# A four-layer attention and FFN program: spline weights made by GpSimd in the attention before, and the spline stage in another order

## The chip, the cores and the metric

The program runs on one core of one Trainium2 chip. A core has TensorE (PE), VectorE (DVE), ScalarE (ACT), GpSimd (POOL) and SyncE (SP, which here only issues DMA transfers). The metric is device time in microseconds; lower is better. All tiles that matter here are fp32.

## The reference

Eight sequences of 100 tokens of 512 pass through four layers, each a cross-attention over 361 context rows and an FFN. What the change touches is in layers 0 to 2:

```python
# layer 0 FFN: 16 experts of width 352, top 4 of 16, capacity 256
mid = silu(einsum('ech,ehi->eci', xg, w_gate)) * einsum('ech,ehi->eci', xg, w_up)
eout = einsum('eci,eih->ech', mid, w_down) * wbuf[..., None]
# layer 1 attention: 16 heads, q and output projections with 8-bit rows
# layer 1 FFN: three 2048 x 512 weights, each a cubic spline through 8134 control points
w = 0.5 * (2*p1 + (p2-p0)*f + (2*p0-5*p1+4*p2-p3)*f**2 + (3*p1-p0-3*p2+p3)*f**3)
inter = silu(x @ gate_w.T) * (x @ up_w.T)
return inter @ down_w.T
# layer 2 FFN: weights rounded to fp8 in blocks of 32
q = (blocks / scales).astype(float8_e4m3fn); return q * scales
```

## The kernel before

Each stage is a block in which every engine has its own program, written out by hand; semaphores order the engines. At a block's end all engines meet. No planner is involved: the order in the code is the order on the engine, and SP's DMA issues wait in one queue like any other instruction.

**Experts (`stage_L0_experts`).** 16 experts of 256 rows make 32 units of 128 rows. TensorE runs for unit u: `gate(u + 1)`, `turn_mid(u)`, `up(u + 1)`, `turn_x(u + 2)`, `down_part(u)`. VectorE makes `product(u)`, which `turn_mid(u)` waits for, and `result(u)`. Besides, the class `Triples` rounds the weights of layer 2's FFN to fp8: 16 triples (768 KB each, two halves each). `scales(n)` (VectorE) needs the loaded triple; GpSimd scales the half, `rounding(n)` is VectorE's, GpSimd's `finish` multiplies back, SP stores the triple to memory. Eight triples are done here, one half in each of units 0 to 15, the others in the column FFN. In units 16 to 23 VectorE quantizes attention weights (`rows8.vector`). SP loads expert 1's weights, the attention's constants (`rows8.sync`: four weights of 1 MB, two contexts, two masks, biases), three triples, and then follows the experts.

**Second attention (`stage_L1_attention`).** A loop over 8 batches. TensorE works on batch b and makes the keys and values of batch n = b + 1 in between: `scores(b, 1)`, `turn_heads(b, 0)`, `keys(n, 0)`, ... `keys(n, 0)` waits for the context tile `cx[n % 2]` (722 KB). SP loads `cx[b]` once the values of b - 2 are made and GpSimd has multiplied that context by the row weights (`multiplied`), then the mask. GpSimd in batch b: negate the next mask, `prod`, bias, four gathers of a later batch's expert rows, and `root(b + 2)`, which waits for VectorE's `measure(b + 2)` near the batch's end. `rows8.w` is free by then.

**Spline stage (`stage_L1_ffn`).** The down weight is made in natural order in four parts of four strips: GpSimd multiplies points by powers, TensorE multiplies by tables (`made`), ScalarE copies one side (`laid`), VectorE lays the other over it (`w_made`, `beyond_border`), SP stores it, and when all is stored GpSimd gathers sixteen strips in another row order. VectorE also measures the eight sequences and normalizes them to `xn`; TensorE transposes these (columns of x, `xT`) and multiplies them by a basis (`moments`). Gate and up weights come from eight tiles of taps: VectorE makes gate's (`gate_weights`), GpSimd up's (`up_weights`), with two tap buffers loaded by SP.

**Column FFN (`stage_columns_ffn`).** Two halves of 400 tokens, 16 chunks of hidden columns each. TensorE runs `gate_up(n)` for a pair of chunks and `down_part` two pairs behind; ScalarE makes `silu`, VectorE `product`. Between them VectorE and GpSimd round the other eight triples, a half per pair. At the half, `turn_y(0)` transposes the result and VectorE's `add` adds it; the summaries of the next layer's recurrence are made there too.

## Time and profile before

| | |
|---|---|
| Median of 3 runs | 2425.5 us (2421.78 to 2426.56) |
| Profiled execution, its own time | 2420.43 us |
| Its span in the trace | 2418.3 us |
| TensorE busy | 2228.2 us (92%), granted clock 0.951 in the mean |
| VectorE busy | 1337.7 us (55%) |
| ScalarE busy | 773.5 us (32%) |
| GpSimd busy | 762.1 us (32%) |
| DMA | 212.69 MB, 88 GB/s in the mean |

The span runs from the first to the last instruction; 2.1 us of the execution's time lie around it. In it the experts stage runs from about 677 to 966 us, the second attention to 1284, the spline stage to 1377 and the column FFN to 1525. A busy share is a mean over stages; what a change in one stage is worth is read from that stage.

### The profile page before, as it was taken

The page shows a single profiled execution, that of the slowest core. Times are in us where ns is not written, and L with a number is a line of the kernel's source. Part 1 is how long each engine was busy: PE and PEld are TensorE (multiplying, and loading weights), DVE is VectorE, ACT ScalarE, POOL GpSimd, SP SyncE. Part 2 cuts the span into 40 slices and gives each one's busy share as a digit, 9 for nine tenths or more (in the row PEclk, how much of TensorE's full clock was granted, in tenths as well). Part 3 has the DMA queues.
Part 4 walks back from the last instruction along what each step waited for, and adds up shares of the span by engine and source line. Part 5 has one row for each costly group of instructions (what it writes and reads, how often), then busy time and mean ns, then how long its engine had stood idle before and what let it go on. Part 6 is the DMA issues. An engine that isn't in the chain of part 4 may idle for free. (4 is left out here: it accounts for less than half of the span.)

```text
span 2418.3 us, 29406 instructions
## 1 busy us (share of the span) xinstructions
PE 2228.2 (92%) x10009; PEld 1178.9 (49%) x10009; DVE 1337.7 (55%) x3440; ACT 773.5 (32%) x2045; POOL 762.1 (32%) x760
## 2 busy tenths in 40 slices
PE   8999999998969999999996498799998899999899
PEld 4455555555436565555553254544443444444454
DVE  5544344206318741476766268867663455555897
ACT  1134344314001111455552111511110456645433
POOL 3655455203203300432112533400000355656100
PEclk9999999998989999899996699999999899999899
DMA  6025300005267853211004622620002211211000
GB/s 199 1 82 187 125 17 13 1 1 161 77 221 262 301 211 120 83 55 32 31 1 152 236 104 92 217 90 5 9 5 67 73 44 52 61 39 48 16 14 15
DMA packets 97353, 212.69 MB, mean 88 GB/s; under 512 B 19060, under 2 KB 37908, under 8 KB 95416
## 3 DMA queue, kind: packets, MB, share of 16 engines
q1 hardware_dynamic: 89784, 193.51, 23.4%
q0 software_dynamic: 7424, 17.32, 2.5%
q8 instruction: 82, 1.34, 0.2%
q14 instruction: 63, 0.52, 0.1%
HBM read 155.70 MB, written 50.14 MB: 85 GB/s over the span
## 5 line engine op out<-in xcount | busy, mean ns | idle before, releaser
L3839 POOL TENSOR_SCALAR a_p<-a_p,a_li 100x257 f32<-100x257 f32 x252 | 188.3, 769 | 110.5 <-DVE a_li L3702 110.5
L633 POOL TENSOR_SCALAR a_shared<-a_shared,a_li 128x361 f32<-128x361 f32 x104 | 131.7, 1266 | 182.4 <-DVE a_li L541 182.4
L3457 PE MATMUL bank<-l_early,a_ctx 128*128 128x512 f32 (+1 forms) x384 | 180.2, 615 | 0.0
L3457 PEld LDWEIGHTS bank<-l_early,a_ctx 128*128 128x128 f32 (+1 forms) x384 | 68.8, 188 | 85.0 <-issue 85.0
L313 PE MATMUL bank<-a_wk,a_ctx 128*128 128x512 f32 (+1 forms) x192 | 94.7, 614 | 9.0 <-DMA a_wk<-in_L_xattn_Wk 5.6
L691 ACT ACTIVATE a_shared<-a_shared,a_nm 128x361 f32<-128x361 f32 x104 | 62.1, 597 | 98.9 <-DVE a_nm L535 98.9
L2721 PE MATMUL bank<-f_h,s_w 128*128 128x400 f32 x256 | 93.2, 519 | 0.0
L2376 ACT ACTIVATE f_sg<-bank 128x512 f32<-128x512 f32 x25 | 14.9, 597 | 238.1 <-PE bank L2159 221.7
L313 PE MATMUL bank<-a_wv,a_ctx 128*128 128x512 f32 (+1 forms) x192 | 90.7, 592 | 0.0
L396 PE MATMUL bank<-a_q_o,a_wq_wo 128*128 128x400 f32 x256 | 88.4, 500 | 0.6 <-issue 0.6
L2326 POOL TENSOR_TENSOR f_rstd<-f_var,half 128x1 f32<-128x1 f32 (+1 forms) x12 | 7.1, 591 | 259.6 <-DVE f_var L2231 259.6
L1295 PE MATMUL bank<-e_wd,e_midT 128*128 128x512 f32 (+1 forms) x192 | 87.9, 593 | 0.6 <-ACT e_midT L1332 0.6
L1559 PE MATMUL bank<-w_ctx,w_wk 128*128 128x361 f32 x256 | 88.2, 489 | 0.0
L2185 PE MATMUL bank<-s_wd,f_hT 128*128 128x512 f32 x192 | 87.4, 599 | 0.0
L1567 PE MATMUL bank<-w_wv,w_ctx 128*128 128x512 f32 (+1 forms) x192 | 87.0, 598 | 0.0
L328 PE MATMUL bank<-a_wq_wo,a_shared 128*128 128x512 f32 x192 | 86.5, 593 | 0.0
L2159 PE MATMUL bank<-s_wgu,f_xT 128*128 128x512 f32 x192 | 84.6, 593 | 0.7 <-ACTq L2366 0.7
L533 DVE MEMSET a_hold<- 1x1 f32 x104 | 6.1, 59 | 141.6 <-PE bank L366 125.4
L2159 PE MATMUL bank<-s_wgu,s_lead 128*128 128x512 f32 x192 | 84.4, 592 | 0.0
L1275 PE MATMUL bank<-e_wu,e_xT 128*128 128x352 f32 x256 | 82.8, 467 | 0.0
L1266 PE MATMUL bank<-e_wg,e_xT 128*128 128x352 f32 x256 | 81.1, 459 | 0.2 <-ACT e_xT L1320 0.2
L1931 ACT ACTIVATE a_p<-a_p,a_nm 100x361 f32<-100x361 f32 x128 | 74.7, 588 | 13.0 <-DVE a_nm L1773 13.0
(498 smaller groups left out, 4863.9 us busy)
## 6 DMA issues: line engine op xcount, KB each, us to landing
slots_x<-zero SPq DMA_DIRECT2D x4, 4096.0 KB, 27.0
s_whole<-in_L_ffn_w SPq DMA_DIRECT2D x24, 512.0 KB, 3.7
e_wg<-in_L_ffn_w_gate SPq DMA_DIRECT2D x16, 704.0 KB, 5.7
e_wu<-in_L_ffn_w_up SPq DMA_DIRECT2D x16, 704.0 KB, 7.9
e_wd<-in_L_ffn_w_down SPq DMA_DIRECT2D x16, 512.0 KB, 4.3
e_xg<-slots_x SPq DMA_DIRECT2D x16, 512.0 KB, 5.4
slots_y<-e_y SPq DMA_DIRECT2D x32, 256.0 KB, 4.6
a_ctx<-in_ctxT SPq DMA_DIRECT2D x30, 256.0 KB, 3.1
```

What stands on the lines that cost most here:

```text
L313: mm = nc.tensor.matmul(R.bank(name, b, c)[0:m, :], cx[:, kc, lo:lo + m], w[:, kc, :], start=(kc == 0), stop=(kc == KC - 1))
L328: mm = nc.tensor.matmul(bank[:], xnT[:, kc, t * P:(t + 1) * P], wq[:, kc, n * D:(n + 1) * D], start=(kc == 0), stop=(kc == KC - 1))
L396: mm = nc.tensor.matmul(R.bank("y", half, m)[:, 0:BY_HALF * S], wo[:, h, m * P:(m + 1) * P], qo[:, half * BY_HALF:(half + 1) * BY_HALF, h, ...
L633: pool.tensor_scalar(p[s % NP], p[s % NP], li[:, b % 2, h:h + 1], None, ALU.mult).then_inc(normed, 1)
L1295: mm = nc.tensor.matmul(b_y[:], midT[u % 2][0:n, c, :], wd[e % 2][0:n, c, :], start=(c == 0), stop=(c == len(IC) - 1))
L1559: mm = nc.tensor.matmul(R.bank("k", b, n)[:, 0:T], wks[:, kc, n * P:(n + 1) * P], cx[b % 2][:, kc, :], start=(kc == 0), stop=(kc == KC - 1))
L1567: mm = nc.tensor.matmul(R.bank("v", b, c)[0:m, :], cx[b % 2][:, kc, lo:lo + m], wvs[:, kc, :], start=(kc == 0), stop=(kc == KC - 1))
L2159: mm = nc.tensor.matmul(banks[u % 2][:], xT[i % 2][:, n, kc, :], w[:, kc, j * D:(j + 1) * D], start=(kc == 0 and n == 0), stop=(kc == KC - ...
L2185: mm = nc.tensor.matmul(b_y[i % 2][:], hT[u % 2][:, n, kc, :], down[:, j * KC + kc, :], start=(j == 0 and kc == 0 and n == 0), stop=(j == ...
L2721: mm = nc.tensor.matmul(b_y[d][:, 0:GT], down[:, f, d * P:(d + 1) * P], h[m % 4][:], start=(f == 0), stop=(f == FC - 1))
L3457: mm = nc.tensor.matmul(bank[0:m, :], columns[:, kc], w[:, kc, :], start=(kc == 0), stop=(kc == KC - 1))
L3839: pool.tensor_scalar(p[g % 2][j][:, lo:hi], p[g % 2][j][:, lo:hi], li[:, h, i:i + 1], None, ALU.mult) \
```

## The change

Four things are edited. (1) GpSimd makes the gate and up weights of the spline FFN in the second attention, one tile of taps in each batch, in `rows8.w`; SP loads the taps, stores the results to memory, and in the spline stage one DMA of 1 MB loads them. (2) The spline stage's order is: measure, normalize, transposes, basis products, and then the down weight. Eight of the sixteen gathers are issued in it and the block doesn't wait for their landing; the other eight are issued by GpSimd at the start of the column FFN, whose `down_part` waits for them by groups of four. (3) Ten triples, not eight, are rounded in the experts stage, in units 4 to 15 and 24 to 31; their loads begin after expert 0, and `scales(0)` stands behind unit 3. (4) At the half of the column FFN `gate_up(PAIRS + 1)` stands ahead of `turn_y(0)`, and two `silu` ahead of `copy_y(0)`. The lines that move the table products behind the basis products on TensorE and ScalarE (the same loops, with a wait for `moved` in part 0), the semaphores and the tile declarations are left out here.

```diff
@@ -1217,8 +1218,6 @@
                 load_gate_up(1)
                 load_down(1)
                 rows8.sync(sp, *weights8)
-                for t in range(3):
-                    triples.load(sp, t)
                 for e in range(NE):
                     more = e + 2 < NE
                     if more:
@@ -1231,11 +1230,16 @@
-                    if 1 <= e <= EARLY_TRIPLES:
-                        triples.store(sp, e - 1)
-                        if e + 2 < EARLY_TRIPLES:
-                            triples.stored(sp, e - 1)
-                            triples.load(sp, e + 2)
+                    if e == 0:
+                        for t in range(3):
+                            triples.load(sp, t)
+                    if e in STORES_AFTER:
+                        t = STORES_AFTER[e]
+                        triples.store(sp, t)
+                        if t + 3 < EARLY_TRIPLES:
+                            triples.stored(sp, t)
+                            triples.load(sp, t + 3)
+                triples.store(sp, EARLY_TRIPLES - 1)
                 for i in range(2):
                     sp.wait_ge(stored[i], 16 * NE)
                 for t in range(EARLY_TRIPLES - 3, EARLY_TRIPLES):
@@ -1358,16 +1362,18 @@
                     dve.tensor_copy(y[u % 2][:], b_y[:]).then_inc(y_made, 1)
 
                 step = Link(dve, stepped)
-                triples.scales(dve, step, 0)
                 product(0)
                 for u in range(U):
                     if u + 1 < U:
                         product(u + 1)
                     result(u)
-                    if u < triples.n:
-                        if u + 1 < triples.n:
-                            triples.scales(dve, step, u + 1)
-                        triples.rounding(dve, step, u)
+                    if u + 1 == ROUNDING_UNITS[0]:
+                        triples.scales(dve, step, 0)
+                    if u in ROUNDING_UNITS:
+                        n = ROUNDING_UNITS.index(u)
+                        if n + 1 < triples.n:
+                            triples.scales(dve, step, n + 1)
+                        triples.rounding(dve, step, n)
@@ -1524,6 +1530,11 @@
+        free = rows8.w[:].rearrange("p i c n -> p (i c) n")
+        by = [free[:, i, :] for i in range(2)]
+        taps = [[free[:, 2 + 2 * i + w, :].rearrange("p (m o) -> p m o", m=4) for w in range(2)] for i in range(2)]
+        taps_in, taps_out = [sem(f"taps_in{i}") for i in range(2)], [sem(f"taps_out{i}") for i in range(2)]
+        spline_made, pool_stepped = sem("spline_made"), sem("pool_steps")
@@ -1540,13 +1551,33 @@
             def _(sp):
+
+                def load_taps(t):
+                    if t >= 2:
+                        sp.wait_ge(taps_out[t % 2], t // 2 * 32)
+                    sp.dma_start(by[t % 2], spline_by[t].rearrange("p m o -> p (m o)")).then_inc(taps_in[t % 2], 16)
+                    for w in range(2):
+                        sp.dma_start(taps[t % 2][w], spline_taps[w, t]).then_inc(taps_in[t % 2], 16)
+
+                def store_weights(t):
+                    sp.wait_ge(spline_made, 2 * t + 2)
+                    for w in range(2):
+                        sp.dma_start(spline_weights[:, w, t, :], taps[t % 2][w][:, 0, :]).then_inc(taps_out[t % 2], 16)
+
+                load_taps(0)
+                load_taps(1)
                 for b in range(2, B):
-
+                    store_weights(b - 2)
+                    load_taps(b)
                     sp.wait_ge(*R.full("v", b - 2, 2))
                     sp.wait_ge(multiplied, b - 1)
                     sp.dma_start(cx[b % 2][:], ctxT[b]).then_inc(c_in[b % 2], 16)
                     sp.wait_ge(maxed, (b - 1) * NH)
                     sp.dma_start(m_in[b % 2][:], mask[b]).then_inc(mk_in[b % 2], 16)
+                for t in range(TILES_W - 2, TILES_W):
+                    store_weights(t)
+                for i in range(2):
+                    sp.wait_ge(taps_out[i], TILES_W // 2 * 32)
@@ -1879,6 +1910,16 @@
+                step = Link(pool, pool_stepped)
+
+                def interpolate(t):
+                    pool.wait_ge(taps_in[t % 2], (t // 2 + 1) * 48)
+                    for w in range(2):
+                        a = taps[t % 2][w]
+                        step(pool.tensor_tensor(a, a, by[t % 2].rearrange("p (m o) -> p m o", m=4), ALU.mult))
+                        step(pool.tensor_tensor(a[:, 0:2], a[:, 0:2], a[:, 2:4], ALU.add))
+                        pool.tensor_tensor(a[:, 0, :], a[:, 0, :], a[:, 1, :], ALU.add).then_inc(spline_made, 1)
@@ -1903,6 +1944,7 @@
                         gather(b + 4)
                     if b + 2 < B:
                         root(b + 2)
+                    interpolate(b)
 
@@ -2573,7 +2616,9 @@
-EARLY_TRIPLES = 8
+EARLY_TRIPLES = 10
+ROUNDING_UNITS = [*range(4, 16), *range(24, 32)]
+STORES_AFTER = {t + 3 if t < 6 else t + 7: t for t in range(EARLY_TRIPLES - 1)}
@@ -2717,8 +2762,10 @@
+                    if m < FC and f % QUADS == 0:
+                        pe.wait_ge(down.arrived[f // QUADS], QUADS * 16)
@@ -2755,9 +2803,9 @@
-                turn_y(0)
                 pe.wait_ge(all_copied, 1)
                 gate_up(PAIRS + 1)
+                turn_y(0)
                 for n in range(PAIRS + 2, 2 * PAIRS + 1):
@@ -2786,8 +2834,10 @@
+                silu(FC)
+                silu(FC + 1)
                 copy_y(0)
-                for m in range(FC, 2 * FC):
+                for m in range(FC + 2, 2 * FC):
                     silu(m)
@@ -2826,42 +2877,58 @@
+                for f in range(FC // 2, FC):
+                    down.gather(pool, f)
                 triples.pool(pool)
@@ -2877,88 +2944,46 @@
-                    def load_taps(t):
-                        if t >= 2:
-                            for n in range(2):
-                                sp.wait_ge(taps_used[n], t - 1)
...
+                        down.store(sp, N * t, N * (t + 1))
+
+                    sp.dma_start(basis[:], w_in["spline_basis"]).then_inc(basis_in, 16)
                     sp.dma_start(tm[:], w_in["spline_terms"]).then_inc(c_in, 16)
                     for t in range(3):
                         load_part(t)
-                    for t in range(2):
-                        load_taps(t)
-                    sp.dma_start(basis[:], w_in["spline_basis"]).then_inc(basis_in, 16)
-                    sp.dma_start(order[:], w_in["spline_order"]).then_inc(basis_in, 16)
+                    sp.dma_start(down.order[:], w_in["spline_order"]).then_inc(order_in, 16)
                     load_part(3)
-                    store_part(0)
-                    load_taps(2)
-                    store_part(1)
-                    load_taps(3)
-                    store_part(2)
-                    load_taps(4)
-                    store_part(3)
-                    for t in range(5, TILES_W):
-                        load_taps(t)
+                    sp.dma_start(weights[:], spline_weights).then_inc(weights_in, 16)
+                    for t in range(PARTS_W):
+                        store_part(t)
...
-                    def up_weights(t):
...
+                    for b in range(B):
+                        root(b)
                     for t in range(PARTS_W):
                         pool.wait_ge(p_in[t % 3], (t // 3 + 1) * 32)
                         pool.tensor_tensor(pts[t % 3][:], pts[t % 3][:], pw[t % 3][:], ALU.mult).then_inc(multiplied, 1)
-                        root(2 * t)
-                        root(2 * t + 1)
-                    for t in range(TILES_W):
-                        up_weights(t)
-                    pool.wait_ge(basis_in, 32)
-                    pool.wait_ge(natural_out, PARTS_W * 16)
-                    for f in range(FC):
-                        pool.indirect_dma_start(wd[:, f, :], None, natural[:, :],
-                                                bass.IndirectOffsetOnAxis(ap=order[:, f:f + 1], axis=0)).then_inc(down_in, 16)
-                    pool.wait_ge(down_in, FC * 16)
+                    pool.wait_ge(order_in, 16)
+                    pool.wait_ge(down.stored, PARTS_W * 16)
+                    for f in range(FC // 2):
+                        down.gather(pool, f)
...
-                    pe.wait_ge(c_in, 16)
...
-                        pe.wait_ge(laid if b < N else w_made, (PARTS_W - 1) * N + b % N + 1)
@@ -3012,24 +3049,14 @@
-                    def gate_weights(t):
...
-                    for t in range(PARTS_W):
-                        measure(2 * t)
-                        measure(2 * t + 1)
-                        beyond_border(t)
+                    for b in range(B):
+                        measure(b)
                     for b in range(B):
                         normalize(b)
-                    for t in range(TILES_W):
-                        gate_weights(t)
-
-        stage_columns_ffn(k, "f1", weights, wd, xT, moments, raw, rounded, early, recurrence)
+                    for t in range(PARTS_W):
+                        beyond_border(t)
+
+        stage_columns_ffn(k, "f1", weights, weights_in, down, xT, moments, raw, rounded, early, recurrence)
```

## Rows read from the trace of the kernel before

**Rows 1.** Busy time by stretch, the second attention; us from the span's start, then length.
```profile
1000.00:1284.00 284.00, 265.81 (x1972) 151.32 (x1972) 190.35 (x599) 154.62 (x448) 68.20 (x50) 0.97 0.11 34
```

**Rows 2.** TensorE's longest waits: line, releaser, us in total, times, longest.
```profile
PE bank L2698 <- PEq L2865: 33.3, 1, 33.3
PE bank L1284 <- DVE e_mid L1352: 22.7, 1, 22.7
```

**Rows 3.** Timeline of TensorE, experts: start, length, instructions.
```profile
682.88 2.53 PE L1266 MATMUL bank<-e_wg,e_xT 128*128 128x352 f32 x8
...
715.87 2.53 PE L1266 MATMUL bank<-e_wg,e_xT 128*128 128x352 f32 x8
...
723.96 2.53 PE L1266 MATMUL bank<-e_wg,e_xT 128*128 128x352 f32 x8
```

**Rows 4.** Timelines of VectorE and TensorE, start and end of the experts.
```profile
706.14 0.95 DVE L2618 TENSOR_REDUCE e_top<-e_triple 128x24 f32<-128x768 f32 x1 [29.73 <-DMA e_triple<-in_L_ffn_triples]
...
716.68 0.94 DVE L2618 TENSOR_REDUCE e_top<-e_triple 128x24 f32<-128x768 f32 x1
...
721.36 0.96 DVE L2629 TENSOR_TENSOR e_v<-e_v,e_c 128x768 f32<-128x768 f32 x1
...
961.80 0.69 DVE L1358 COPY e_y<-bank 128x512 f32<-128x512 f32 x1 [3.05 <-PE bank L1295]
...
965.65 2.00 PE L1470 MATMUL bank<-ident,w_wide 128*100 128x128 f32 x8 [3.88 <-PEq L1195]
```

**Rows 5.** DMA issues: size each and median us from issue to landing.
```profile
rounded<-e_triple SPq DMA_DIRECT2D x8, 768.0 KB, 6.6
...
rounded<-f_triple SPq DMA_DIRECT2D x8, 768.0 KB, 3.2
...
w_ctx<-in_ctxT SPq DMA_DIRECT2D x8, 722.0 KB, 4.1
...
out<-l_early SPq DMA_DIRECT2D x6, 256.0 KB, 2.0
```

**Rows 6.** Timelines of GpSimd and TensorE, `root(7)` and `keys(7, 0)` of the second attention.
```profile
1212.76 0.57 POOL L1880 TENSOR_TENSOR a_rstd<-a_var,half 100x1 f32<-100x1 f32 x1 [24.81 <-DVE a_var L1739]
...
1223.54 2.67 PE L1559 MATMUL bank<-w_ctx,w_wk 128*128 128x361 f32 x8
```

**Rows 7.** The taps' instructions on GpSimd: ns min/median/max, first and last start.
```profile
L2923 POOL TENSOR_TENSOR s_taps<-s_taps,s_by x8: 1260/1772/1781, 1310.2 to 1349.7; 128x512 f32<-128x512 f32 x8
L2924 POOL TENSOR_TENSOR s_taps<-s_taps x8: 722/724/787, 1311.5 to 1351.5; 128x256 f32<-128x256 f32 x8
L2925 POOL TENSOR_TENSOR s_u<-s_taps x8: 452/455/805, 1312.3 to 1352.3; 128x128 f32<-128x128 f32 x8
```

**Rows 8.** Stretches behind TensorE's restart: the third number from the end is the granted clock.
```profile
965.00:967.00 2.00, 1.35 (x6) 1.38 (x7) 0.17 (x1) 1.37 (x2) 0.62 (x1) 0.50 0.00 0
...
971.00:973.00 2.00, 2.00 (x7) 1.22 (x6) 0.00 (x0) 0.99 (x3) 1.70 (x2) 0.84 0.57 146
```

**Rows 9.** Timelines of the spline stage, and the gathers' first and last start.
```profile
1285.54 0.69 DVE L2990 BATCH_NORM_STATS2 s_stats<-res 100x6 f32<-100x512 f32 x1 [1.64 <-PEq L80]
...
1286.55 0.68 DVE L2990 BATCH_NORM_STATS2 s_stats<-res 100x6 f32<-100x512 f32 x1
...
1309.59 2.56 DVE L3012 COPY_PREDICATED s_w<-s_beyond,bank 128x512 f32<-128x512 uint8 x4
...
1321.46 22.55 PE L2966 MATMUL bank<-s_xT,s_basis 128*128 128x400 f32 x64
...
L2938 POOL DMA_INDIRECT s_w<-spline_down,s_order x16: 944/946/1069, 1353.1 to 1372.0; - x16
```

**Rows 10.** Timeline of VectorE in the column FFN, its first rounding and the half.
```profile
1386.90 0.50 DVE L2626 TENSOR_SCALAR f_c<-f_v 128x768 int32<-128x768 int32 x1
...
1453.01 2.46 DVE L2807 TENSOR_TENSOR res<-res,bank 100x512 f32<-100x512 f32 x4
```

**Rows 11.** The gathers of the second attention: ns min/median/max.
```profile
L1874 POOL DMA_INDIRECT a_got<-slots_y,slots_of x32: 1007/1012/1507, 966.4 to 1119.6; - x32
```

## Prediction on record

> **What bounds the kernel now.** I read the busy time by stretch first, then TensorE's waits, then the timelines where they are long. TensorE is the bound: it is 92% busy on the page, and in the second attention it works 265.8 of 284.0 us at a granted clock of 0.97 while VectorE, ScalarE and GpSimd have room [rows 1]. So only what stops TensorE, or starts it later, costs time. Its two longest waits are both in stages that the change touches: 33.3 us ahead of the first column product of the spline FFN, and 22.7 us at the first expert's `turn_mid(0)` [rows 2]. The reader should ask of each part: does it take one of these away, and what is late next.
>
> **Triples in the experts stage: start.** VectorE's first instruction there is `triples.scales(0)`, ahead of `product(0)`, and it sits idle 29.73 us until the first triple lands at 706.14 [rows 4]; TensorE stands behind it. The change puts `scales(0)` after unit 3 and the triple loads after expert 0. Nothing then holds `product(0)`. `gate(1)` began at 682.88 and a unit lasts 723.96 - 715.87 = 8.09 us, so `gate(2)` begins at 690.97 in place of 715.87 [rows 3]: -24.9 us (22.7 of wait and 2.2 of slow restart). What is late next are transfers. From the sizes in the code, 9.5 MB went ahead of VectorE's 706.14 (expert 1's weights 2.16 MB, the attention's constants 6.6, one triple 0.79), which is 324 GB/s over 29.4 us. Expert 2's rows and gate/up weights now make 10.7 MB: 33 us, so 709.7 against a need at 682.9 + 3 x 8.09 = 707.2 (or later loads, behind the three triples, 16.3 MB: 727 against 723.3). The rate there was no better than this mean, but the small constants may have pulled it down. Between 0 and 5 us; I take +1, since most of these are wide rows.
>
> **Triples in the experts stage: end.** `ROUNDING_UNITS` now ends with unit 31, so VectorE rounds after the last tiles. Before, `result(31)` ran at 961.80 and all engines restarted at 965.65 [rows 4]. One `scales` and `rounding` take 721.36 + 0.96 - 716.68 = 5.6 us [rows 4]. The idle of 3.05 us in that row says that VectorE's `result(30)` ended at 958.7; `scales(19)` and `rounding(18)` push `result(31)` to 964.4 to 965.0; `rounding(19)` (4.1 us of the 5.6) ends at 969.2; GpSimd's `finish`, a 128x768 product, is 1.3 to 1.9 us by the 128x512 one that runs alone in 1.26 [rows 7], 1.5 taken: 970.7; the store of 768 KB lands in 3.2 us at the median [rows 5], which with issue and the block's end makes 975.2. That is +9.5 us. Bounds: +8.5, and +13 at 6.6 us, the median of the same store amid this stage's loads [rows 5]. TensorE idles through it, so its restart is slow in both kernels alike.
>
> **The second attention.** GpSimd gets `interpolate(b)` after `root(b + 2)`: six instructions, each half 1.26 to 1.78, 0.72 and 0.45 us [rows 7], so 5.4 to 6.2 with their steps; 5.6 taken. GpSimd has room, and the DVE instructions that it can slow have slack. But SP's loop is one queue, and ahead of the load of `cx[b + 2]` it now waits for the weights of tile b, stores them, waits until both stores landed, and issues three taps loads. Behind that wait stand `cx[b + 2]` and the mask. Count from `root`: 1212.76 + 0.57 = 1213.33 [rows 6]. Interpolation: 1218.9. Two stores issued in 0.4 us steps, the second landed 2.0 us later (the nearest row, an output store of 256 KB [rows 5]): 1221.4. Three loads issued, then the context load, issued at 1222.8; alone it lands in 4.1 us [rows 5]: 1226.9, and with 768 KB of taps just ahead 1227.4. `keys(b + 2, 0)` wants it at 1223.54 [rows 6]. TensorE waits 3.9 us; bounds 3.0 and 5.4. The delay doesn't shrink by itself: the next `measure` and `root` come after a product that TensorE runs behind these keys, so they move with the wait. Six loads are of this kind (batches 2 to 7). Before, that load had to wait only for `prod`, at the batch's start.
>
> After an idle of 3.9 us TensorE restarted at a granted clock of 0.50, the lower of its levels (1.2 of 2.4 GHz), and was back between 971 and 973 (mean 0.84), some 5.7 us later [rows 4, 8]. Half speed for 4 to 5.7 us of work costs 2.0 to 2.9; I take 2.2 (the row's wait is as long as mine; nothing if the wait is shorter than whatever drops it). So 6 x (3.9 + 2.2) = +36.6 us; 6 x 3.0 = 18 below, 6 x (5.4 + 2.9) = 50 above.
>
> **The spline stage.** Before: tables, then columns of x, then the products with the basis, which end at 1321.46 + 22.55 = 1344.0; then TensorE waits for GpSimd's and VectorE's taps and sixteen gathers, 1.26 us apart (1353.1 to 1372.0) [rows 9, 2]. Now: eight `measure` at 1.01 us from 1285.54 end at 1293.6; columns and transposes take what they took (1312.1 to 1321.5, 9.4 us) and perhaps 1 more beside GpSimd's products: 1304; basis products to 1326.6; the first tables 2 us; four copies of a part 2.56 us, sixteen 10.2 and hand-overs [rows 9]: 1340. The stores of 4.2 MB and the 1.3 MB of weights and borders share the queue from 1332; at 324 GB/s they need 17 us: 1349. Eight gathers: 1359. The block then ends without waiting for them, TensorE starts at 1359.3 against 1377.3: -18 us. If the stores drain a third faster it is -22; if the chain is longer by two gathers, -15. The removed taps (8 of each engine and 24 loads) are inside this number, and the single load of the finished weights is long landed.
>
> **The column FFN.** GpSimd issues eight gathers (10 us) ahead of `triples.pool`, so `rounding(0)`, before at 1386.90, 9.6 us after the start [rows 10], can begin only at 11.5, and the products behind it on VectorE with it; TensorE had little slack: +1.6 (0 to 4). At the half, `gate_up(PAIRS + 1)` now stands ahead of `turn_y(0)`: VectorE's `add` began at 1453.01 [rows 10] right after the summaries and now waits for those 1.6 us and the copy: +2.4, as the wait for `silu` that follows is behind these adds and a rounding. Two triples fewer save nothing: in the last pairs TensorE is back to back. +4 together.
>
> On these gathers a rule speaks against the change. The slowest of the 32 gathers of the second attention took 1.51 us beside a median of 1.01 [rows 11]. The Trainium skill (SBUF — State Buffer, section SBUF: two separate sides) says that a GpSimd-issued DMA is starved of descriptors while VectorE holds the shared port, and gives 0.62 us growing to about 3.1. This row shows a growth of half, not fivefold, so the trace bears it out only weakly.
>
> **Sum.** -24.9 + 1 + 9.5 + 36.6 - 18 + 4 = +8.2 us on the profiled execution's 2420.4, 2428.6. That execution is 5.1 us under the median 2425.5 of the runs, so in runs: 2434.
>
> **Rivals.** (1) The other side: the waits in the attention are at their lower bound, 3.0 us, and too short for the clock to fall. Then 18 in place of 36.6: -10.4, 2415. It decides at 6 x (wait + clock) = 28.4, that is 4.7 us a batch. For it: all but 0.9 us of the wait hangs on durations taken near their middle. Against it: the row with 3.9 us of idle fell. (2) The context loads are not late at all, because stores and taps overlap more than I think: -28.4, 2397. Against it: the window between `root` and need is 10.2 us, and interpolation and one landing already take 9.7. (3) Everything slow: 5.0 us waits with 2.9 of clock (47), experts' loads 5 late: +23, 2448. For it: the queue's taps are ahead of the context. (4) Gathers in the column FFN starved by VectorE as by the rule, all eight at the slowest one's 1.51 us and a gap of 0.3 [rows 11]: 4.5 us more before `rounding(0)`, +12.7, 2438. Against it: VectorE has little to do in those first 10 us. By the page's factor of five they would take 40 us, and the time would be some 2464.
>
> **Chances.** Forecast 0.50, its own range 2427 to 2441; (1) 0.27; (2) 0.06; (3) 0.13; (4) 0.04. From 2410 to 2452 holds all but (2) and the far ends of (1) and (3). A measurement tells 0.2%, 4.9 us, from no change. Faster: (2), most of (1), a little of the forecast: 0.27. Same: the lower part of the forecast and the rest of (1): 0.22. Slower: 0.51.
>
> **What would show it.** In the new profile: no wait of TensorE at `turn_mid(0)`; 8 to 13 us idle of all engines at the end of the experts; at each `keys(n, 0)`, n = 2 to 7, a wait of 3 to 5 us ended by the context load, and a granted clock of 0.5 behind it; the column FFN's start 15 to 22 us nearer to the attention's end. The prediction is wrong if those keys don't wait, or if the load runs ahead of the taps.

## The result, and the profile after

| | before | after |
|---|---|---|
| Median of 4 runs each | 2425.5 us (2421.78 to 2426.56) | 2449.3 us (2446.47 to 2453.24) |
| Profiled execution / its span | 2420.43 / 2418.3 us | 2446.47 / 2444.0 us |
| TensorE busy, granted clock | 2228.2 us, 0.951 | 2237.5 us, 0.952 |

The changed kernel takes 1.0097 times as long (95% interval 1.0079 to 1.0115): 23.8 us slower, where the prediction said 8.2. The page doesn't show it: TensorE's busy time grew by 9 us, and the mean clock is the same. The stages do. Each row of this table is one profiled execution, cut at the same events: TensorE's first product of the experts, its first of the second attention, VectorE's first `measure` of the spline stage, TensorE's first of the column FFN, the first transpose of its `turn_y(1)`, and the end.

| us | experts begin | experts | attention | spline | column FFN | rest |
|---|---|---|---|---|---|---|
| before | 678.0 | 287.6 | 319.9 | 91.8 | 144.3 | 896.7 |
| after | 682.5 | 275.1 | 365.0 | 78.8 | 145.9 | 896.8 |
| difference | +4.5 | -12.5 | +45.1 | -13.0 | +1.6 | +0.1 |
| predicted | 0 | -14.4 | +36.6 | -18 | +4 | 0 |

TensorE's longest waits in the changed kernel (line, releaser: us in total, times, longest) answer to [rows 2]:

```profile
PE bank L1590 <- DMA w_ctx<-in_ctxT: 27.7, 6, 5.3
PE bank L2743 <- PEq L2932: 25.1, 1, 25.1
PE bank L2983 <- DVE s_xn L3041: 16.5, 4, 15.9
PE bank L1476 <- PEq L1196: 12.4, 1, 12.4
```

The 22.7 us at `turn_mid(0)` are gone and the 33.3 us are 25.1. In their place stand six waits for a context, and 12.4 us at the attention's first product where 3.88 stood. Those two grew by 27.7 + 8.6 us against the 22.7 + 8.2 that went, which would be 5.4 us slower; a wait's price is more than its length, as the clock will show. The third line is the start of the spline stage in its new order.

**Experts.** TensorE's timeline of the changed kernel (start, length, instructions, idle before), which answers to [rows 3] and the last of [rows 4]:

```profile
687.34 2.53 PE L1270 MATMUL bank<-e_wg,e_xT 128*128 128x352 f32 x8
...
695.42 2.53 PE L1270 MATMUL bank<-e_wg,e_xT 128*128 128x352 f32 x8
...
703.50 2.53 PE L1270 MATMUL bank<-e_wg,e_xT 128*128 128x352 f32 x8
...
711.49 0.66 PE L1258 MATMUL bank<-ident,e_xg 128*128 128x128 f32 x4 [2.76 <-DMA e_xg<-slots_x]
...
715.33 1.13 PE L1270 MATMUL bank<-e_wg,e_xT 128*128 128x352 f32 x3 [0.60 <-issue]
...
957.59 2.00 PE L1476 MATMUL bank<-ident,w_wide 128*100 128x128 f32 x8 [12.45 <-PEq L1196]
```

`gate(2)` follows `gate(1)` after 8.08 us: the whole 24.9 us are won. Then one wait comes, for expert 2's rows; the next `gate` is at 715.33, not 711.58 (703.50 + 8.08), so it costs 3.75. At the end all engines stand still for 12.45 us, where they stood for 3.88.

**Attention.** GpSimd, SP and TensorE around the second of the late contexts:

```profile
1065.52 0.57 POOL L1911 TENSOR_TENSOR a_rstd<-a_var,half 100x1 f32<-100x1 f32 x1 [15.68 <-DVE a_var L1770]
...
1070.79 0.46 POOL L1921 TENSOR_TENSOR w_w<-w_w 128x128 f32<-128x128 f32 x1
...
1071.27 0.81 SPq L1565 DMA_DIRECT2D spline_weights<-w_w  x2
1073.40 0.33 SPq L1558 DMA_DIRECT2D w_w<-in_spline_by  x1
1073.77 0.92 SPq L1560 DMA_DIRECT2D w_w<-in_spline_taps  x2
1074.79 0.37 SPq L1574 DMA_DIRECT2D w_ctx<-in_ctxT  x1
...
1081.78 4.67 PE L1590 MATMUL bank<-w_ctx,w_wk 128*128 128x361 f32 x8 [5.35 <-DMA w_ctx<-in_ctxT]
```

Read it as a chain: root, interpolation (5.2 us), stores (0.8) and their landing (1.3), three loads of taps, the context's issue, and 7.0 us later the keys that waited for it. The same keys took 2.67 us before [rows 6] and take 4.67 here. The stretches behind the wait say why (the third number from the end is the granted clock):

```profile
1082.00:1084.00 2.00, 2.00 (x4) 1.20 (x5) 0.00 (x0) 0.00 (x0) 2.00 (x2) 0.50 0.00 0
1084.00:1086.00 2.00, 2.00 (x5) 1.09 (x5) 0.00 (x0) 0.00 (x0) 2.00 (x2) 0.55 0.00 0
1086.00:1088.00 2.00, 2.00 (x32) 1.38 (x31) 0.98 (x2) 0.56 (x1) 1.49 (x3) 1.00 0.00 0
```

TensorE is busy all the time, but at the lower of its levels (0.50, 1.2 of 2.4 GHz). The same stands behind the shortest of the six waits, 3.50 us ahead of the keys at 1124.72, where the clock is 0.50 from 1124 to 1130:

```profile
1126.00:1128.00 2.00, 2.00 (x5) 1.12 (x4) 0.00 (x0) 0.00 (x0) 2.00 (x1) 0.50 0.00 0
```

**Spline stage.** Timelines of VectorE, GpSimd, TensorE and SP in the changed kernel; the first `measure` is at 1322.54:

```profile
1331.16 4.06 DVE L3041 TENSOR_SCALAR s_xn<-res,s_stat,s_rstd 100x4 f32<-100x4 f32 x1
1335.14 0.54 DVE L3039 TENSOR_SCALAR s_xn<-res,s_stat,s_rstd 100x512 f32<-100x512 f32 x1
1335.71 0.29 DVE L3041 TENSOR_SCALAR s_xn<-res,s_stat,s_rstd 100x4 f32<-100x4 f32 x1
...
1331.50 3.70 POOL L2972 TENSOR_TENSOR s_points<-s_points,s_powers 128x512 f32<-128x512 f32 x3
...
1335.28 1.71 PE L2983 MATMUL bank<-ident,s_xn 100*128 100x100 f32 x8 [15.95 <-DVE s_xn L3041]
...
1370.95 6.85 SPq L2896 DMA_DIRECT2D spline_down<-s_w  x4
...
1397.06 0.95 POOL L2899 DMA_INDIRECT s_w<-spline_down,s_order  x1 [0.30 <-issue]
...
1401.33 1.70 PE L2743 MATMUL bank<-s_xT,s_gate_up 32*128 32x400 f32 x4 [25.09 <-PEq L2932]
```

An instruction on 100x4 elements takes 4.06 us, its twin 0.29: it begins 0.34 us before the record of GpSimd's three products and ends with the last of them, at 1335.2. The last gather of the stage ends at 1398.0, TensorE's column products start 3.3 us later.

**Column FFN.** GpSimd's last gather, VectorE's first rounding and TensorE behind the half:

```profile
1410.99 0.95 POOL L2899 DMA_INDIRECT s_w<-spline_down,s_order  x1 [0.30 <-issue]
...
1413.48 1.82 DVE L2671 TENSOR_SCALAR f_c<-f_v 128x768 int32<-128x768 int32 x1 [2.09 <-issue]
...
1472.16 3.60 PE L2791 MATMUL bank<-l_early,l_u 128*8 128x512 f32 x8
...
1488.43 1.71 PE L2743 MATMUL bank<-s_xT,s_gate_up 32*128 32x400 f32 x8 [8.38 <-ACT f_sg L2824]
```

Rounding starts 12.2 us after the stage, not 9.6 [rows 10]. From the summaries to the wait's end are 16.3 us; before they were 13.9 (1448.76 to 1462.63).

### The profile page after: what moved, and what is told of

The parts are those of the page before. It is cut to its first block and busy times, and to the rows that moved or that the text cites. A ratio compares the mean times of both kernels' runs of the same rounds, so it can differ in the third digit from the quotient of the medians.

```text
span 2444.0 us, 29422 instructions
## 1 busy us (share of the span) xinstructions
PE 2237.5 (92%) x10009; PEld 1186.7 (49%) x10009; DVE 1316.4 (54%) x3424; ACT 773.8 (32%) x2045; POOL 776.2 (32%) x784
## 5 line engine op out<-in xcount | busy, mean ns | idle before, releaser
L1590 PE MATMUL bank<-w_ctx,w_wk 128*128 128x361 f32 x256 | 100.0, 541 | 27.7 <-DMA w_ctx<-in_ctxT 27.7
L2688 POOL TENSOR_TENSOR e_v<-e_triple,e_inv 128x768 f32<-128x768 f32 x20 | 33.1, 1654 | 206.8 <-DVE e_inv L2665 206.8
L1590 PEld LDWEIGHTS bank<-w_ctx,w_wk 128*128 128x128 f32 x256 | 53.5, 220 | 59.5 <-DMA w_ctx<-in_ctxT 28.7
L534 DVE MEMSET a_hold<- 1x1 f32 x104 | 6.1, 59 | 141.5 <-PE bank L367 125.4
```

Source lines behind the costliest of these rows:

```text
L1590: mm = nc.tensor.matmul(R.bank("k", b, n)[:, 0:T], wks[:, kc, n * P:(n + 1) * P], cx[b % 2][:, kc, :], start=(kc == 0), stop=(kc == KC - 1))
```

## The experiments

Twelve runs were made, in four groups on four chips, each beside runs of the kernel before on the same chip; ratios are against those, and are what can be compared between groups. "The length of a stage" is that of the table above.

### Is it the context's place in SP's queue?

```diff
                 for b in range(2, B):
-                    store_weights(b - 2)
-                    load_taps(b)
...
                     sp.dma_start(m_in[b % 2][:], mask[b]).then_inc(mk_in[b % 2], 16)
+                    store_weights(b - 2)
+                    load_taps(b)
```

> The changed kernel with one edit: in the second attention SP loads the context and the mask of batch b ahead of the stores of the finished weights and the loads of taps. Theory 1 (the context stands behind the taps in SP's queue): the waits of TensorE at keys(2..7, 0), 27.7 us in 6, go altogether; the clock stays up behind them, so TensorE's busy time in the stage falls by some 10 of the 14.4 us that it grew; the stage shrinks from 363.9 to 322 to 328 us, and the time from 2449.3 to 2409 (2403 to 2415). Theory 2 (GpSimd's interpolation itself slows the other engines at the shared port): the waits at the keys go but others of 2 to 3 us a batch on VectorE's results come in their place: 2420 to 2430. Theory 3 (the slow clock is not due to these waits): only the 27.7 us go, 2421.

Measured: 2403.13 us, ratio 0.9896 (0.9878 to 0.9914): the changed kernel with this one edit is faster than the kernel before. The attention is 322.7 us, and no wait for a context is left. Busy times of the whole stage, first of the changed kernel, then of this one (PE is the first number after the length):

```profile
957.59:1322.54 364.95, 310.71 (x2096) 176.87 (x2096) 194.57 (x631) 165.89 (x468) 121.39 (x112) 0.91 0.18 54
```

```profile
957.86:1280.52 322.66, 297.13 (x2096) 170.18 (x2096) 208.54 (x631) 165.96 (x468) 122.70 (x112) 0.95 0.21 61
```

The queue order costs 42.3 us: 28.7 of idle time and 13.6 in which the same 2096 matmuls ran slower, 2.3 us for each of the six waits. Theories 2 and 3 fall: no other wait of that size came in place of these, and the slow clock went with them. What GpSimd's work costs by itself is the rest to the kernel before, 322.7 - 319.9 = 2.8 us.

The second kernel puts the context between the stores and the taps, so that it waits for the interpolation and not for the landing:

```diff
                     store_weights(b - 2)
-                    load_taps(b)
...
                     sp.dma_start(m_in[b % 2][:], mask[b]).then_inc(mk_in[b % 2], 16)
+                    load_taps(b)
```

> The changed kernel with one edit: SP stores the finished weights of batch b - 2 first, then loads context and mask of batch b, then waits for the stores and loads the taps. The context's issue comes earlier by the stores' landing and three issues, some 3.1 us, and has no taps in flight ahead. Theory 1: the wait at the keys falls from 4.6 us to 1 to 2 us each, 6 to 12 us in all, and so short a wait leaves TensorE's clock up: busy time as in the run with the context first, and the time 6 to 12 us above that run, some 2418. Rival (the clock falls behind any wait): the same waits but 2 to 3 us of slow clock each, some 2430. Rival (the transfer itself is slow here, not its place in the queue): waits stay at 4 us or more, 2440 or above.

Measured: 2411.31 us, ratio 0.9926 (0.9908 to 0.9943), 8.2 above the run with the context first. The waits of TensorE in the attention, and the whole stage:

```profile
PE bank L1590 <- DMA w_ctx<-in_ctxT: 4.7, 6, 1.5
```

```profile
953.96:1283.30 329.34, 297.74 (x2096) 170.23 (x2096) 198.01 (x631) 165.95 (x468) 123.98 (x112) 0.95 0.20 59
```

Six waits of 0.8 us in the mean, the longest 1.5, and a busy time that is 0.6 us off that of the run without waits: behind none of them does the granted clock leave 1.00, while the wait of 5.35 us had some four us of work at half clock behind it and the one of 3.50 more than five. The prediction's rival (1) had waits of 3.0 us without a slow clock. That short waits can go without one is shown for 0.4 to 1.5 us; at 3.0 us no context wait was measured, and the nearest, 3.50, had the slow clock. Nor is the length of the wait all that decides, as the attention's end will show.

### The experts' stage by itself

The kernel before with the hunks of the experts stage (and the guard `if n < triples.n` in the column FFN) and nothing else.

> The kernel before with the edits of the experts stage alone (loads of triples after expert 0, scales(0) behind unit 3, ten triples in units 4 to 15 and 24 to 31, six left for the column FFN). Theory 1 (the terms add): no wait at turn_mid(0), some 12 us idle at the stage's end, the stage 276.4 us in place of 288.9, nothing gained in the column FFN: 2425.5 - 12.5 = 2413. Rival 1: the stage ahead (routing), which came 4.5 us later in the changed kernel, belongs to this edit or to the program's length: 2417 to 2418. Rival 2: six triples in place of eight free VectorE and GpSimd in the column FFN and give 3 us or more: 2410.

Measured: 2412.5 us, ratio 0.9943 (0.9926 to 0.9961), 14.3 us faster. Its experts take 274.4 us (13.2 less than before), attention and spline stage are as before (319.5 and 91.5), the column FFN 141.5 in place of 144.3. Theory 1 holds for the experts. The 2.8 us of the column FFN are hardly the two triples that left it. They lie in its first half (from the stage's start to the summaries' second product), of which these are the whole rows, first of the kernel before, then of this run:

```profile
1377.31:1448.76 71.45, 68.42 (x296) 36.73 (x297) 47.58 (x69) 9.79 (x21) 23.48 (x15) 0.90 0.41 149
```

```profile
1366.40:1435.41 69.01, 65.07 (x297) 34.84 (x297) 47.58 (x69) 9.77 (x21) 23.47 (x15) 0.95 0.43 154
```

VectorE and GpSimd do the same work in both; TensorE is busy 3.4 us longer in the first, at a clock of 0.90 against 0.95. The first profile of before has a stretch of half clock there in which TensorE did not idle (shown at the end of this text); this run has none. Other profiles differ there by as much (below).

### Four more edits at once: one in the experts, one in the column FFN, two in the spline stage

```diff
-ROUNDING_UNITS = [*range(4, 16), *range(24, 32)]
-STORES_AFTER = {t + 3 if t < 6 else t + 7: t for t in range(EARLY_TRIPLES - 1)}
+ROUNDING_UNITS = [*range(4, 16), *range(22, 30)]
+STORES_AFTER = {t + 3 if t < 6 else t + 6: t for t in range(EARLY_TRIPLES - 1)}
...
+                    if e == NE - 1:
+                        triples.store(sp, EARLY_TRIPLES - 1)
                     store(2 * e + 1)
...
-                triples.store(sp, EARLY_TRIPLES - 1)
...
+                turn_y(0)
                 pe.wait_ge(all_copied, 1)
                 gate_up(PAIRS + 1)
-                turn_y(0)
...
+                    pool.wait_ge(xn_made, B)
                     for t in range(PARTS_W):
                         pool.wait_ge(p_in[t % 3], (t // 3 + 1) * 32)
...
+                    sp.dma_start(weights[:], spline_weights).then_inc(weights_in, 16)
                     load_part(3)
-                    sp.dma_start(weights[:], spline_weights).then_inc(weights_in, 16)
```

(ScalarE's two `silu` go behind `copy_y(0)` again.)

> The changed kernel with the context first and four more edits: the rounding's last eight halves in units 22 to 29 and the last triple's store ahead of the last result's store; the order at the half of the column FFN as before the change; GpSimd's products of points and powers in the spline stage held until all eight sequences are normalized; the load of the finished weights ahead of the fourth part's. Theory: from the context-first time (2409) the end of the experts gives 5 to 7 us (idle of TensorE 12.5 to some 6), the half 2.4, the products 3.5 (the instruction of 4.06 us becomes 0.29; TensorE's transposes begin 3.7 earlier), the weights' load 2 to 3 (stores land earlier): 2395 (2391 to 2400). Rival: the spline stage's length is set by the stores' drain alone, so that the products give only what they move ahead of it and the load gives nothing: 2398. Rival: rounding in units 22 and 23, beside the last rows8 instructions, delays product and the keys of two units: 2400.

Measured: 2387.55 us, ratio 0.9837 (0.9818 to 0.9857), 15.6 under the run with the context first; the expected 2391 to 2400 were counted from 2409 for that run, which took 2403. By stage: the experts 266.7 us in place of 274.7 (-8.0), with all engines idle for 3.30 us at the end; the spline stage 73.5 in place of 79.1 (-5.6); from the summaries to the end of the wait 13.9 us again. VectorE and TensorE at the start of the spline stage, where GpSimd now holds its products back:

```profile
1281.18 0.29 DVE L3041 TENSOR_SCALAR s_xn<-res,s_stat,s_rstd 100x4 f32<-100x4 f32 x1
1281.37 0.54 DVE L3039 TENSOR_SCALAR s_xn<-res,s_stat,s_rstd 100x512 f32<-100x512 f32 x1
...
1281.52 1.71 PE L2983 MATMUL bank<-ident,s_xn 100*128 100x100 f32 x8 [12.17 <-DVE s_xn L3041]
```

The 4.06 us are 0.29, and TensorE waits 12.17 us in place of 15.95. So it was the collision of VectorE with GpSimd. The Trainium skill (SBUF — State Buffer, section SBUF: two separate sides) says that the two share a pair of ports as an exclusive lock for one whole instruction; the trace agrees with the lock, but here VectorE stood through three products of GpSimd, not one.

The 5.6 us that the spline stage gained are not simply these 3.8 handed on. The last copy of the down weight ends 54.8 us after the stage's start in this run and 54.9 in the changed kernel. What shrank is the time from the last store's issue to the first gather, 10.4 us there and 4.7 here. Two edits could do that: the stores begin 3.2 us earlier, because the basis products end earlier, and the 1 MB of finished weights no longer stands just ahead of them. No run separates the two.

### Was the new order of the spline stage worth anything?

From the kernel of the four edits: table products, `laid`, `beyond_border` and measures first, then normalizing, transposes and basis products, as before the change; all sixteen gathers in this stage, none in the column FFN, and the finished weights' load behind the stores. The taps stay out of it.

```diff
+                    for t in range(PARTS_W):
+                        measure(2 * t)
+                        measure(2 * t + 1)
+                        beyond_border(t)
-                    for b in range(B):
-                        measure(b)
                     for b in range(B):
                         normalize(b)
-                    for t in range(PARTS_W):
-                        beyond_border(t)
...
-                    for f in range(FC // 2):
+                    for f in range(FC):
                         down.gather(pool, f)
```

> The kernel of the four more edits, with the spline stage in the order of the kernel before: table products and down weight first (measures between them), then columns of x, transposes and basis products, and all sixteen gathers in this stage; gate and up weights stay made in the attention. Theory 1 (with the taps gone from the stage, what is late is the chain of down weight, stores, gathers, and it should run beneath the 23 us of basis products): tables end 26 us after the stage's start as before, the stores have landed by 40, sixteen gathers end by 60, the basis products at 58.5; the stage 59 to 62 us in place of 73.5, and the column FFN's first half 1.9 us shorter: 2387.5 - 14 = 2373 (2370 to 2378). Rival (the order of the change is what shortened the stage, since measures, normalizing and products now share VectorE in a worse order): 73 us or more, 2387 or above. Rival (the stores drain late as before behind other transfers): gathers end at 68, 2381.

Measured: 2372.44 us, ratio 0.9769 (0.9756 to 0.9782), 15.1 under the four edits on another chip, and 16.7 under the run `spread` on the same chip, which holds the four edits (below). GpSimd's first and last gather, and TensorE:

```profile
1304.09 1.07 POOL L2896 DMA_INDIRECT s_w<-spline_down,s_order  x1 [7.98 <-DMA spline_down<-s_w]
...
1323.02 0.95 POOL L2896 DMA_INDIRECT s_w<-spline_down,s_order  x1 [0.30 <-issue]
```

```profile
1305.96 22.58 PE L2999 MATMUL bank<-s_xT,s_basis 128*128 128x400 f32 x64
1329.38 0.94 PE L2744 MATMUL bank<-s_xT,s_gate_up 32*128 32x400 f32 x4 [0.84 <-PEq L2929]
```

Sixteen gathers end at 1324.0, beneath the basis products (to 1328.5), and TensorE waits 0.84 us where it waited 19.7 to 25.1. The stage is 58.6 us long. What shortened it in the change was that the taps left it; the reordering, which looks like part of the same step, cost 15 us of that again, since it put the one chain that leaves TensorE idle (copies, stores, their landing, gathers) behind everything that could cover it.

### The rest of the experts' start

Two kernels ask what expert 2's rows wait for. One takes the four edits and loads one triple after each of experts 0, 1 and 2 (`if e < 3: triples.load(sp, e)`):

> The kernel of the four more edits, with the first three triples loaded one each after experts 0, 1 and 2, not all three after expert 0. Theory: TensorE's wait of 2.76 us for expert 4's rows goes, which stood behind those 2.3 MB, and the experts' stage is 3 us shorter: 2384.5. Rival: the wait only moves behind the later loads, or VectorE's scales(2) waits for the second triple and with it product: 2387.5 or up to 2390.

Measured: 2389.11 us, ratio 0.9842 (0.9828 to 0.9855); the experts take 266.68 us, and 266.69 without it, and TensorE still waits 2.37 us for these rows (the expectation calls them expert 4's; unit 4 is expert 2's). The triples aren't it. The other, with the tables first, moves `rows8.sync(sp, *weights8)` (6.6 MB) behind expert 2:

> The kernel with the tables first, with one more edit: SP loads the attention's constants (6.6 MB) after expert 2, not ahead of expert 2's rows. Theory: the 2.8 us for which TensorE waits for expert 2's rows (and 1.1 around it) are due to these constants ahead in the queue, as the estimate of the prediction had it, and not to the triples: the experts' stage is 262.8 to 263.5 us in place of 266.63, the time 3 to 4 us less: 2369. Rival (loads later in the stage only move the lateness to other experts' weights or to the quantizing in unit 16): the stage stays at 266 or grows: 2372 to 2376.

Measured: 2375.1 us, ratio 0.9787 (0.9768 to 0.9806), so no gain. The wait for expert 2's rows is gone: from 689.53 to 754.18 every `gate` begins 8.08 us after the last. But at 764.11 stands this:

```profile
764.11 1.11 PE L1260 MATMUL bank<-ident,e_xg 128*128 128x128 f32 x4 [4.71 <-DMA e_xg<-slots_x]
```

It is expert 5's rows, behind the same constants; the stage is 269.7 us. Half of the theory held, and the rival decided the time. How the constants delay the rows shows in SP's queue: of the burst's thirteen issues the last five, four biases and the decay table, take 8.9 us here (743.40 to 752.34), and only then are expert 5's rows issued; in the changed kernel they took 12.1 (687.16 to 699.29), ahead of expert 2's. The next pair therefore spreads them, one constant behind each of experts 1 to 13, against a kernel that differs in nothing else:

```diff
-                rows8.sync(sp, *weights8)
+                constants = rows8.loads(sp, *weights8)
...
+                    if 1 <= e <= len(constants):
+                        dst, src, sem = constants[e - 1]
+                        sp.dma_start(dst, src).then_inc(sem, 16)
```

> The kernel with the tables first and the last tile's interpolation at the start of batch 7, the constants where the change has them; it is the one that the next run is compared with. Theory: experts' stage 266.6, attention 319.5 to 320.5, 2371. Rival: nothing gained at the attention's end, 2372.5.

> The same, with the attention's thirteen constants loaded one behind each of experts 1 to 13. In the run that loaded them all after expert 2 the wait for expert 2's rows was gone and one of 4.7 us stood at expert 5's rows, behind them. Theory (it is the burst of 6.6 MB that makes rows late, wherever it stands): no wait for rows at all, the experts' stage 262.5 to 263.5 us, the time 3 to 4 us below the run beside it, 2367 to 2368. Rival (the stage's transfers, 0.71 of the DMA engines busy in the mean, leave no room, so that any load costs a wait): 266 us or more.

Measured: 2368.07 us, ratio 0.9763 (0.9749 to 0.9778), and 2365.91 us, ratio 0.9756 (0.9743 to 0.9769). The experts take 266.5 and 263.2 us. TensorE waits for no rows any more; its longest waits in the stage are

```profile
PE bank L1488 <- PEq L1196: 3.3, 1, 3.3
PE bank L1262 <- PEq L808: 1.0, 1, 1.0
PE bank L1292 <- DVE e_mid L1360: 0.9, 1, 0.9
```

The 3.3 us are plain in the two traces and too few for the two intervals to tell apart. This is the version with the lowest median, 59 us below the kernel before on the same chip.

### The last tile's interpolation, and the noise of one profile

At the attention's end of the changed kernel GpSimd's interpolation of tile 7 runs beside VectorE's output quantizing:

```profile
1297.24 1.48 DVE L1409 TENSOR_SCALAR a_otmp<-a_o,a_inv 100x512 f32<-100x512 f32 x1
1298.75 0.83 DVE L1410 TENSOR_SCALAR a_otmp<-a_otmp 100x512 f32<-100x512 f32 x1
...
1300.24 0.35 PE L1605 MATMUL bank<-identb,a_oq 100*128 100x100 bf16 x4 [2.65 <-DVE a_oq L1411]
```

> The kernel of the four more edits, with the last tile's interpolation moved to the start of batch 7 (ahead of prod), where GpSimd idles 26 us. Theory: at the end of the attention VectorE's a_otmp takes 0.5 and 0.4 us in place of 1.48 and 0.83, TensorE waits 1.2 in place of 2.65 for a_oq and the clock stays up behind it, so the attention is 319.9 us in place of 322.8: 2384.7. Rival (the same collision moves to another instruction of VectorE on the path): no change, 2387.5.

Measured: 2389.34 us, ratio 0.9829 (0.9815 to 0.9842), the same as without it. The attention is 320.5 us in place of 322.8, so the stage did gain 2.3, but no median shows it. VectorE's instruction takes 0.48 us and TensorE's wait is 1.11 us, as expected; that the clock stays up behind it was not: it is 0.50 from 1250 to 1254 in this run, where the kernel before keeps 1.00 behind a wait of 1.22 us at the same product. A second try, on the kernel with the late constants:

> The same with the last tile's interpolation at the start of batch 7. Theory: both edits give their stage's part, attention 319.5 to 320.5 in place of 321.6: 2367 to 2368. Rival: the attention's end gains nothing outside single profiles: as the run with the late constants, 2369.

Measured: 2373.62 us, ratio 0.9785 (0.9769 to 0.9801), against 0.9787 without; attention 319.6 and 322.0. The third pair, `tables_first` and `last_tables`, has 321.6 and 320.5. The stage gains 1.1 to 2.4 us in single profiles, two profiles of the kernel before differ there by 1.3 (below), and medians of five don't show it: the sign is the same three times, the size is not known. The last run asks how far single profiles can be trusted:

> The kernel before once more, for a second profile of it. In the first, the experts began at 678.0 us and in five profiles of changed kernels at 679.5 to 683.2, though nothing ahead of them was edited. Theory: that is the spread of single executions (stretches of half clock that fall where they will), and this profile shows the experts' start anywhere from 678 to 683 and the length of the first half of the column FFN at 69.0 to 71.5. Rival: the kernel before always starts them at 678, and the edits cost 4 us there.

Measured: 2432.74 us, span 2430.6. The experts begin at 686.0, eight us later than in the first profile; experts, attention, spline stage and column FFN take 287.6, 318.6, 92.2 and 145.0 us, within 1.3 of the first each, the rest 901.3 against 896.7. The theory expected 678 to 683 and was too narrow; the rival falls, as the changed kernels' profiles begin them at 677.2 to 684.7. The +4.5 us ahead of the experts are the spread of executions.

## Why the prediction came out as it did

The direction, its main mechanism and its place were right: six late contexts, whose price is a wait and a slow clock, eat what the other parts give. The size was not: the edited stages gave +21.2 us by the profiles where the sum said +8.2, and 2449.3 lies outside the forecast's own 2427 to 2441, in the part of the stated range that rival (3) held. The mis-sized terms are the attention (+8.5), the spline stage (+5) and the experts' loads (+2.8). Point by point:

- **Experts' start.** -24.9 held (32.99 us from `gate(1)` to `gate(2)` became 8.08). "Loads +1 (0 to 5)" was 3.75. The estimate behind it (709.7 against a need at 707.2) had the wait almost right (2.5 us; measured 2.76), and I then took 1 against it; the constants ahead are shown to be the cause. The other 1.0 of the 3.75 is slower work and issue behind the wait.
- **Experts' end.** +9.5 was 8.6; a rounding that ends two units earlier, with its store ahead of the last result's, takes 8.0 of it back.
- **Attention.** +36.6 was 45.1, the largest miss. The clock's term was right (6 x 2.2 = 13.2; measured 13.6). Waits were 4.6 us in the mean, not 3.9 (+4.3 in all). The chain up to the context's issue was even shorter than priced (8.7 us from `root`'s end in five of the six, not 9.5), but the keys began 6.2 us after that issue in the mean (5.2 to 7.0), where I gave 4.1 alone and 0.5 for the taps ahead: the medians of the landing of these six contexts are 4.1 before, 4.8 with the taps behind it and 6.2 with them ahead. That term was under-sized. The rest is 1 us of other idle time and 2.8 of interpolation, which I had at nothing because "the DVE instructions that it can slow have slack": in batch 7 they have none, and moving that one tile gave 1.1 to 2.4 of it back.
- **Spline stage.** -18 was -13.0. Measures, tables and the last copy came when forecast (54.9 us after the start, forecast 54.5). The stores had landed 2 us later than forecast: the basis products, which the port lock had held up by 3.8 (I gave it 1), ended 43.0 us after the start (forecast 41.1), and the queue of the finished weights and the stores began 1.4 us late. And 3 us lie between the last gather and the next stage's first product, for which I gave 0.3; before, they were hidden in the same row as the landing. By the two edits in this stage 5.6 us of it came back.
- **Column FFN.** +4 was +1.6, but that is an accident of the profile of before, whose first half (71.5 us) has the stretch of half clock (the second profile of before, 71.1 us, has a shorter one). Against `experts_only`, which rounds the same six triples there and has no such stretch, the first half is 1.8 us longer (70.8 and 69.0; forecast 1.6 for the gathers ahead of the rounding, which starts 2.6 later) and the second 2.6 (75.0 and 72.5; forecast 2.4). That makes +4.4, so both terms stood about as priced, as far as single profiles tell.
- **Rivals.** Rival (3), all slow, with 47 us for the attention and the loads 5 late, gave 2448 and is nearest to what happened: 45.1 for its 47, and loads 3.75 late for its 5. That its total fits to 1.3 us is in part luck: the waits were 4.6 and the clock 2.3 (not 5.0 and 2.9), the spline stage lost 5 us that it did not have, and the profiled execution's +26.0 holds 4.5 us of spread ahead of the experts. Rival (1) needs waits that are too short for the clock; at 0.4 to 1.5 us they are, at 3.5 to 5.35 they aren't, and its own 3.0 did not occur. Rival (2) would have needed 4.6 us that weren't there. Rival (4) fell: the eight gathers in the column FFN took 0.94 to 0.95 us each, 0.30 apart, beside VectorE's work.

What none of the prediction's parts asked is whether the new order of the spline stage is good. The prediction took the chain of stores and gathers as given and priced it, and the price was nearly right, but the kernel's own first order would have hidden it.

## What to carry to other kernels

Work that is free on its engine is not free in the queue that feeds it: put a transfer that the bound engine needs ahead of every wait that belongs to side work, and price such a wait with the slow clock behind it. When work leaves a stage, ask anew which chain ends it and start that chain first. A burst of loads that is moved only moves its victim; spread it.

## What was unexpected of the hardware

- A VectorE instruction on 100x4 elements took 4.06 us beside three back-to-back GpSimd products of 128x512 (3.70 us in all): it got no turn between them. With the products held back it took 0.29.
- TensorE's granted clock also falls with no idle time ahead. In the first profile of before, stretches at the summaries, with TensorE busy throughout from 1432 on (32 products of 8 columns each began at 1436.7, just ahead of the fall):

```profile
1440.00:1444.00 4.00, 4.00 (x9) 2.35 (x10) 0.00 (x0) 0.74 (x4) 0.00 (x0) 0.50 0.00 0
1444.00:1448.00 4.00, 4.00 (x11) 2.13 (x10) 0.00 (x0) 0.00 (x0) 0.00 (x0) 0.74 0.00 0
```

  In the run with the context first the same products ran at 1.00. Where such stretches fall differs from one execution to the next; the column FFN of one and the same code was 139.8 and 143.3 us long in two profiles.
- How long an issue holds SP's queue depends on what was queued ahead of it. The issue of one of the constants, a bias laid out over 100 partitions, took 5.56 us at the end of the burst, while one of a 1 MB weight near its start took 0.44. It is not the bias's own form: in `constants_apart`, where it stands alone, the same issue took 0.37. First the changed kernel, then that run:

```profile
684.40 0.44 SPq L1445 DMA_DIRECT2D w_wk<-in_L_xattn_wk  x1
...
690.88 5.56 SPq L1452 DMA_DIRECT2D w_bo<-in_L_xattn_bo  x1
```

```profile
881.66 0.37 SPq L1240 DMA_DIRECT2D w_bo<-in_L_xattn_bo  x1
```
